# Loads and stores of the first tile spread over two DMA queues, and picks and gathers moved

## The chip, the cores and the metric

The kernel runs on one core of a Trainium2 chip. The metric is the device time of one execution in microseconds (us), lower is better. On the core TensorE (PE) multiplies matrices, VectorE (DVE) and GpSimd (POOL) do elementwise work, ScalarE (ACT) copies and applies functions, and SyncE (SP) only issues DMAs. ScalarE and GpSimd issue DMAs too. DMAs that SP issues appear in the profile as queue q1, those of ScalarE as q10, the gathers of GpSimd as q0.

## The reference

A recommendation tower: 32 embedding tables are looked up for 1024 rows, three layers of a compressed interaction network run over them, and a small dense network follows.

```python
e = stack([tbl_m[ids[:, m]] for m in range(32)], axis=1)       # B=1024, M=32, D=16
x0 = xk = e
for W in (W0, W1, W2):                                         # (32, 32 or 64, 64)
    xk = relu(einsum('bmd,bhd,mhk->bkd', x0, xk, W))           # (B, 64, D)
    outs.append(sum(xk, axis=2))
h = concatenate(outs + [dense_ctx], axis=1)                    # (B, 208)
h = relu(h @ W_top1 + b_top1); h = relu(h @ W_top2 + b_top2)
y = h @ W_top3
```

All arithmetic is in float32.

## The kernel before, in words

The batch is cut into eight tiles of 128 rows (i = 0 to 7), each tile into two sides (A and Bs) of 64 rows. A **phase** is one layer of one side of one tile, written (i, layer, side). The list PHASES (line 59) sets the order of all phases on all engines: (0,0,A), (0,1,A), (0,0,Bs), (0,2,A), (0,1,Bs), (1,0,A), (0,2,Bs), (1,0,Bs), (1,1,A), (1,1,Bs), (1,2,A), (2,0,A), (1,2,Bs), (2,0,Bs), (2,1,A) and so on.

A phase is a row of **steps**. In a step VectorE multiplies a 128 x 1024 tile: the previous layer's values, which ScalarE has laid into two pairs of PSUM banks (xk, one for each of two "turns"), by one **slot** of x0rep, which holds rows of x0 repeated over partitions (line 1119). TensorE then multiplies the product z by a piece of the layer's weights and adds it up in a PSUM bank acc (line 768). A phase of layer 0 has four steps, which use slots 0, 1, 2 and 1 again (in (0,0,A) in the order 0, 2, 1, 1); one of layer 1 or 2 has sixteen, which use the slots 0 to 7 twice. Of those sixteen, two to five products are made by GpSimd (line 569) into z_pool. VectorE's products go round a ring of six buffers (RING), GpSimd's round one of four: a product waits until TensorE is through with the step that had its buffer. When a phase is over, ScalarE takes acc as relu into xk_copy (line 870) and layer_out (line 876), VectorE sums layer_out over d (line 1092), and xk_copy feeds the next layer of the same side (lines 832, 851, 856). In layer 0 TensorE adds squares times w0d ahead of the last step (line 764); the squares are loaded as rows of x0 (load_rows, line 426) and squared by ScalarE (line 812).

**How x0 gets there.** The embeddings of a tile are gathered into emb[:, i % 2] (128 rows x 32 x 16). SP stores them to the DRAM buffer x0_rows, and loads from there the slots (load_x0, line 433, 512 KB each), the layouts lay (load_lay, line 420, 512 KB each) and the rows (load_rows, 128 KB). For tile 0 this is done by halves, even and odd embeddings (save_first, line 461): a half is stored by two DMAs, of 16 and of 8 rows of emb, in pieces of 64 bytes, 3072 in all. Side A's slots 0, 2, 4 and 6 are loaded behind the even half, slots 1, 3, 5 and 7 behind the odd one. For tile 0, side A, the layouts aren't loaded; TensorE turns and selects the rows (turn_rows, select_rows), with a copy by ScalarE between them (copy_rows, line 791, one for each half). Later tiles: save_x0 (line 412), then load_side (line 440) for A and Bs. x0rep has three groups of eight slots, used in turn by the sides.

**Gathers.** Most embeddings come by indirect DMAs that GpSimd issues (line 518). Those of tiles 0 and 1 stand at the start; those of tiles 2 to 7 stand between its products, so many a phase as later_gathers (line 141) says: 6 or 10 a phase, and by the table IN_PHASE (line 137) for tile 2: 4 in (0,1,A), 6 in each of (0,2,A), (0,1,Bs) and (0,2,Bs), 5 in each of (1,1,A) and (1,1,Bs). Of tiles 0 and 1 some embeddings from small tables are **picked** instead: the tables are loaded whole, TensorE multiplies them by one-hot matrices, and VectorE masks and sums (pick_rows, line 1056). There are ten picks, 0 to 9, six of them for tile 0. Picks 0 to 6 stand ahead of the phases on VectorE; the table `between` (line 1088) puts number 7 ahead of step 1 of phase (0,0,A), number 8 ahead of its step 2 and number 9 ahead of phase (0,1,A).

**Weights.** w0 is loaded in 16 small DMAs. w1 and w2 are loaded by ScalarE's queue (load_w, line 777) in eight straight DMAs (STRAIGHT: four pieces of two; 64 KB or 32 KB each) and in four of 32 KB (WRAPPED) from a DRAM copy with wrapped rows, w1_wrap or w2_wrap. The copies are made from DRAM to DRAM by two DMAs of 128 KB each (make_wrap, line 382). TensorE starts phase (0,1,A) when all twelve w1 loads have landed, and (0,2,A) when all of w2 have. The w2 loads stand in ScalarE's program behind the second fill of phase (0,1,A) and wait there for slot 7 and for w2_wrap.

**ScalarE's order in the opening:** table loads; w0 loads; copy_rows(0); four w0 loads; straight w1 pieces 0 and 1; copy_rows(1); pieces 2 and 3; square(0, A); the w1_wrap loads; then the phases. **SP's order:** save_first(0); two w0 loads; slots 0, 2, 4, 6; two w0 loads; save_first(1); wait for it; slot 1; rows; slots 3, 5, 7; make_wrap for w2; load_side(0, Bs), which is rows, a layout, slots 0 and 1, a layout, slots 2 to 7; the dense network's weights (about 0.9 MB); then tile 1.

Each engine works through its own program in order, so a DMA issue that waits holds everything behind it on that engine.

Of the kernel before, what the change touches and what calls it, by code (L numbers as in the profile page):

```python
# [17 lines left out]
P = 128  # L18
# [118 lines left out]
IN_PHASE = {(0, 1, A): 4, (0, 2, A): 6, (0, 1, Bs): 6, (0, 2, Bs): 6, (1, 1, A): 5, (1, 1, Bs): 5}  # L137
# [63 lines left out]
FIRST_SAVES = 4  # L201
# [10 lines left out]
def build(nc, ids, ctx_t, tables, sel, ident, w0a, w0b, w0d, w1, w2, wt1, bt1, wt2, bt2, wt3, out):  # L212
    with ExitStack() as stack:
# [89 lines left out]
        saved_first = sem("saved_first")  # L303
# [83 lines left out]

        def load_lines(queue, by_act, g):

            for m in of_group(g)[0]:  # L390
                if (m in LOADED_BY_ACT) == by_act:
                    queue.dma_start(lines[:, ALL_PICKED.index(m), 0:per_line(m) * D],
                                    tables[m].rearrange("(p j) d -> p (j d)", p=LINES)).then_inc(lines_in[g], 16)

        @block.sync
        def _(sp):
# [20 lines left out]
            def columns(i, side):  # L417
                return (i * SIDES + side) * WIDE

# [12 lines left out]

            def load_x0(i, side, slot):

                g = (i * SIDES + side) % X0_GROUPS
                src = bass.AP(x0_rows, slot * PITCH + columns(i, side),
                              [[2 * PITCH, GROUPS], [0, PER_GROUP], [1, WIDE]])
                sp.dma_start(x0rep[:, g, slot, :], src).then_inc(x0_in[g][slot], 16)

            def load_side(i, side):  # L440
# [8 lines left out]
                for slot in range(SLOTS):  # L449

                    bi, bs = divmod(i * SIDES + side - X0_GROUPS, SIDES)
                    if bi >= 0:
                        sp.wait_ge(z_ready, slot_users(bi, bs, slot, "dve", DVE_COUNT))
                        used = slot_users(bi, bs, slot, "pool", POOL_COUNT)
                        if used:
                            sp.wait_ge(z_pool_ready, used)
                    load_x0(i, side, slot)
                    if slot == 1 and i == 0:
                        load_lay(i, side, 1)

            def save_first(odd):

                sp.wait_ge(gathered_first[odd], 16 * len(FIRST_GATHERS[odd]))
                sp.wait_ge(picked_out, PICKED_EVEN if odd == 0 else len(PICKED))
                for lo, hi, row in ((0, M, odd), (0, X_ROWS - M, M + odd)):
                    dst = bass.AP(x0_rows, row * PITCH, [[D, P], [2 * PITCH, (hi - lo) // 2], [1, D]])
                    sp.dma_start(dst, emb[:, 0, lo + odd:hi:2, :]).then_inc(saved_first, 16)

            save_first(0)
            sp.wait_ge(w0_twice_in, 32)  # L470
            load_w0(sp, W0_LOADS, W0_LOADS + 2)
            sp.wait_ge(saved_first, 32)
            for slot in range(0, SLOTS, 2):
                load_x0(0, A, slot)
            load_w0(sp, W0_LOADS + 2, TILES0 * P // M)
            save_first(1)
            sp.wait_ge(saved_first, 64)
            for slot in range(1, SLOTS, 2):
                load_x0(0, A, slot)
                if slot == 1:  # L480
                    load_rows(0, A)
            make_wrap(sp, w2_wrap, w2, w2_wrap_in)
# [33 lines left out]
        def _(pool):  # L516
# [23 lines left out]
            def gather_later(j, m):  # L540

                if m == 0:

                    if j == 2:
                        pool.wait_ge(idx_in, 16)
                        pool.wait_ge(saved_first, 16 * FIRST_SAVES)
# [229 lines left out]
        def _(act):  # L776
# [27 lines left out]
            load_w(w1_sb, w1.tensor, TILES, w1_in, STRAIGHT[:2])  # L804
            copy_rows(1)
            load_w(w1_sb, w1.tensor, TILES, w1_in, STRAIGHT[2:])
# [9 lines left out]
            load_w(w1_sb, w1_wrap, WRAP, w1_in, WRAPPED)  # L816

# [162 lines left out]
        def _(dve):  # L980
# [104 lines left out]
            between = {1: 7, 2: 8, 4: 9}  # L1085
# [10 lines left out]
            for n, (i, layer, side) in enumerate(PHASES):  # L1096
                g = i * SIDES + side
                filled = [False, False]
                if n == 1:
                    pick_rows(between[len(STEPS[0])])  # L1100
# [6 lines left out]
                for c, (k, (_, _, bank, other)) in enumerate(mine):  # L1107
                    count = DVE_COUNT[n, k]
                    if n == 0 and k in between:
                        pick_rows(between[k])  # L1110
# [81 lines left out]
```

## Time and profile before

| | us |
|---|---|
| median of 3 runs (lowest, highest) | 632.28 (631.21, 635.13) |
| the profiled execution | 633.34 |
| its span | 631.5 |
| VectorE busy in the span | 577.9 (92%) |
| TensorE busy in the span | 586.0 (93%) |
| GpSimd busy in the span | 497.1 (79%) |
| ScalarE busy in the span | 349.7 (55%) |
| mean DMA rate over the span | 151 GB/s |
| granted TensorE clock, mean | 0.97 |

All rows come from the one profiled execution, and times in them count from its span's start. Matmul ends are modelled, so a busy TensorE is not TensorE at its peak. A row of a timeline is: start us, duration us, engine, line, operation, out <- in, shapes, count, and in brackets the idle time ahead of it with what ended it. Rows that follow one another on an engine are merged, so the start of a merged row is that of its first instruction. "SPq" and "ACTq" rows are DMA issues: their duration is the engine's time for issuing, not the transfer. A wait put down to a DMA may have had several semaphores; the one that came last is named.

### The profile page before, as it was taken

Reading aid. Unit: us, or ns where it says so; the run is one execution under the profiler, and the core shown is the slowest. Engines: PE = TensorE matmul, PEld = TensorE weight load, DVE = VectorE, ACT = ScalarE, POOL = GpSimd, SP = SyncE. Lnnn points to the kernel's source line nnn. Section 1 sums busy time; section 2 is a strip of 40 time slices with the busy share of each in tenths; the row PEclk is TensorE's granted clock in tenths of the full one; section 3 lists DMA queues with packets and bytes.
Section 4 is the critical chain, followed back from the end, with each engine's and each line's share of the span. In section 5 each row is a group of like instructions: output and inputs, shape, how many; then the busy total and the mean of one; then the engine's idle time right before and its main releaser. Section 6 shows DMA issues by size and latency. Waiting matters only on the chain.

```text
span 631.5 us, 8730 instructions
## 1 busy us (share of the span) xinstructions
PE 586.0 (93%) x3126; PEld 215.7 (34%) x3126; DVE 577.9 (92%) x582; ACT 349.7 (55%) x535; POOL 497.1 (79%) x349
## 2 busy tenths in 40 slices
PE   3852789999999999999999999999999999999998
PEld 3730222222343224323343224322343224333444
DVE  6746669899999999999999999999999999999993
ACT  0105165455766657535766657536756666756741
POOL 6753549899988998899888988898888896568770
PEclk8796699999999999999999999999999999999999
DMA  4789979990399918995499927992599838950000
GB/s 107 139 162 234 225 126 226 237 229 3 34 237 246 209 5 158 235 233 97 53 237 230 207 17 174 254 247 38 93 234 235 164 27 224 294 167 1 1 2 2
DMA packets 89342, 95.36 MB, mean 151 GB/s; under 512 B 59613, under 2 KB 68354, under 8 KB 89298
## 3 DMA queue, kind: packets, MB, share of 16 engines
q1 hardware_dynamic: 79086, 91.06, 63.9%
q0 software_dynamic: 7104, 1.83, 4.3%
q10 hardware_dynamic: 3108, 1.90, 1.2%
q8 instruction: 25, 0.41, 0.3%
q14 instruction: 19, 0.16, 0.1%
HBM read 91.35 MB, written 3.94 MB: 151 GB/s over the span
## 4 chain that ended last, share of the span: by engine, by line
PE 25%; DVE 23%; issue 5%; ACT 1%; DVEq 0%
PE acc L768 22%; DVE z L1119 22%; DVE row_sums L1092 1%; PE top L605 1%; ACT xk L832 0%; ACT xk L851 0%; PE top L596 0%; PE top L593 0%; PE acc L764 0%; ACT xk L856 0%; PE acc L645 0%; PE xk L633 0%; PE xk L625 0%; PE top L580 0%; DVEq L1117 0%
## 5 line engine op out<-in xcount | busy, mean ns | idle before, releaser
L1119 DVE TENSOR_TENSOR z<-xk,x0rep 128x1024 f32<-128x1024 f32 x457 | 523.7, 1236 | 30.3 <-DMA x0rep<-x_rows 9.5
L768 PE MATMUL acc<-z,w_sb 128*64 128x512 f32 x1828 | 434.5, 601 | 31.0 <-DMA w_sb<-w_wrap 15.0
L569 POOL TENSOR_TENSOR z_pool<-x0rep,xk_copy 128x1024 f32<-128x1024 f32 x119 | 283.3, 2381 | 59.4 <-PE acc L768 41.1
L518 POOL DMA_INDIRECT emb<-tbl,idx x222 | 212.9, 959 | 58.7 <-issue 48.5
L768 PEld LDWEIGHTS acc<-z,w_sb 128*64 128x64 f32 x1828 | 124.6, 137 | 306.0 <-issue 165.3
L856 ACT ACTIVATE xk<-xk_copy 32x1024 f32<-32x1024 f32 x128 | 130.5, 1019 | 92.9 <-DVE z L1119 88.4
L768 PE MATMUL acc<-z_pool,w_sb 128*64 128x512 f32 x476 | 122.6, 593 | 0.4 <-POOL z_pool L569 0.4
L870 ACT ACTIVATE xk_copy<-acc 64x512 f32<-64x512 f32 x128 | 75.2, 588 | 8.2 <-PE acc L768 6.7
L851 ACT ACTIVATE xk<-lay 128x1024 f32<-128x1024 f32 x15 | 15.4, 1028 | 75.3 <-DVE z L1119 75.3
L768 PEld LDWEIGHTS acc<-z_pool,w_sb 128*64 128x64 f32 x476 | 33.8, 137 | 65.7 <-issue 62.1
L832 ACT ACTIVATE xk<-xk_copy 128x1024 f32<-128x1024 f32 x31 | 31.9, 1028 | 14.1 <-DVE z L1119 13.7
L1092 DVE TENSOR_REDUCE row_sums<-layer_out 128x32 f32<-128x512 f32 x47 | 32.8, 697 | 0.0
L812 ACT ACTIVATE squares<-squares 32x1024 f32<-32x1024 f32 x16 | 16.8, 1050 | 28.7 <-DMA squares<-x_rows 16.0
L876 ACT ACTIVATE layer_out<-acc 128x512 f32<-128x512 f32 x47 | 27.8, 591 | 2.7 <-PE acc L768 1.9
L888 ACT ACTIVATE in<-row_sums 64x32 f32<-64x32 f32 x94 | 21.3, 227 | 4.1 <-DVE row_sums L1092 3.1
L677 PE MATMUL acc<-x0rep 125*128 125x160 f32 (+1 forms) x68 | 15.2, 394 | 6.3 <-DMA x0rep<-tbl 6.3
L832 ACT ACTIVATE xk<-lay 128x1024 f32<-128x1024 f32 x15 | 15.4, 1028 | 4.2 <-DMA lay<-x_rows 4.0
L764 PE MATMUL acc<-squares,w0d_sb 128*64 128x512 f32 x64 | 17.5, 625 | 0.3
L677 PEld LDWEIGHTS acc<-x0rep 125*128 125x128 f32 x68 | 13.3, 272 | 8.8 <-DMA x0rep<-tbl 6.8
L605 PEld LDWEIGHTS top<-h,wt_sb 128*64 128x64 f32 x224 | 12.7, 137 | 4.0 <-issue 4.0
L1039 DVE TENSOR_TENSOR x0rep<-acc,mask 128x480 f32<-128x480 f32 (+1 forms) x10 | 6.6, 665 | 7.7 <-PE acc L677 7.7
L605 PE MATMUL top<-h,wt_sb 128*64 128x128 f32 x224 | 13.4, 273 | 0.0
(67 smaller groups left out, 126.5 us busy)
## 6 DMA issues: line engine op xcount, KB each, us to landing
x0rep<-x_rows SPq DMA_DIRECT2D x128, 512.0 KB, 20.8
lay<-x_rows SPq DMA_DIRECT2D x30, 512.0 KB, 7.0
emb<-tbl,idx POOLq DMA_INDIRECT x222, 3.6
squares<-x_rows SPq DMA_DIRECT2D x16, 128.0 KB, 20.5
x_rows<-emb SPq DMA_DIRECT2D x7, 256.0 KB, 4.6
x_rows<-emb SPq DMA_DIRECT2D x9, 128.0 KB, 6.3
w_wrap<-w SPq DMA_DIRECT2D x4, 128.0 KB, 9.7
w_sb<-w ACTq DMA_DIRECT2D x8, 64.0 KB
```

The costliest lines, as they stand in the source:

```text
L518: pool.indirect_dma_start(out=emb[:, i % 2, m, :], out_offset=None, in_=tables[m], in_offset=bass.IndirectOffsetOnAxis(ap=idx[:, i, m:m + ...
L569: pool.tensor_mul(z_pool[:, (count - 1) % POOL_RING, :], x0rep[:, g % X0_GROUPS, slot, :], xk_copy[:, side, :]).then_inc(z_pool_ready, 1)
L605: last = pe.matmul(top[halves[half], m * P:(m + 1) * P], wt2_sb[:, k, columns_of(m, half)], h1[:, k, :], start=(k == 0), stop=(k == F1 // ...
L677: op = pe.matmul(acc[:, ACC_AT[q], t * n * D:(t + 1) * n * D], hots[:, q % HOTS, t * P:(t + 1) * P], lines[:, ALL_PICKED.index(m), 0:n * D ...
L768: mm = pe.matmul(bank[c * H:(c + 1) * H, :], w[:, tile, :], src[:, c * COLS:(c + 1) * COLS], start=(k == 0), stop=last)
L832: act.activation(xk[:, 0, :], src, ACT.Copy).then_inc(xk_ready[0], 1)
L856: op = act.activation(xk[q * Q:(q + 1) * Q, 1, :], xk_copy[other * Q:(other + 1) * Q, side, :], ACT.Copy)
L870: op = act.activation(xk_copy[half * H:(half + 1) * H, side, c * COLS:(c + 1) * COLS], bank[c * H:(c + 1) * H, :], ACT.Relu)
L876: act.activation(layer_out[:, n % OUTS, :], bank, ACT.Relu).then_inc(acc_taken, 1)
L888: op = act.activation(dst[:, at:at + ROWS], row_sums[c * H:(c + 1) * H, i % 2, row, :], ACT.Copy)
L1092: dve.tensor_reduce(row_sums[:, i % 2, SUM_ROWS.index((layer, side)), :], layer_out[:, n % OUTS, :].rearrange("p (b d) -> p b d", d=D), AX ...
L1119: dve.tensor_mul(z[:, (count - 1) % RING, :], xk[:, bank, :], src).then_inc(z_ready, 1)
```

## The change

It has five parts.

1. save_first takes the queue as an argument, and the semaphore saved_first becomes one for each half. The odd half is stored from ScalarE's queue, behind straight w1 pieces 0 and 1 and ahead of copy_rows(1).
2. Slots 1 and 3 of side A are loaded from ScalarE's queue, behind copy_rows(1) and a wait for the odd store, ahead of straight w1 pieces 2 and 3. SP loads slots 0, 2, 4 behind the even store; then, behind the odd store, the rows and slots 5, 6, 7.
3. make_wrap for w2 moves from SP (behind slot 7) to ScalarE, behind the w1_wrap loads, which follow square(0, A).
4. Pick 8 goes ahead of phase (0,1,A), pick 9 ahead of its step 4.
5. The gathers of tile 2: none in (0,1,A), 7 instead of 5 in each of (1,1,A) and (1,1,Bs).

```diff
-IN_PHASE = {(0, 1, A): 4, (0, 2, A): 6, (0, 1, Bs): 6, (0, 2, Bs): 6, (1, 1, A): 5, (1, 1, Bs): 5}
+IN_PHASE = {(0, 1, A): 0, (0, 2, A): 6, (0, 1, Bs): 6, (0, 2, Bs): 6, (1, 1, A): 7, (1, 1, Bs): 7}
...
-        saved_first = sem("saved_first")
+        saved_first = [sem(f"saved_first{odd}") for odd in range(2)]
...
+        def save_first(queue, odd):
+
+            queue.wait_ge(gathered_first[odd], 16 * len(FIRST_GATHERS[odd]))
+            queue.wait_ge(picked_out, PICKED_EVEN if odd == 0 else len(PICKED))
+            for lo, hi, row in ((0, M, odd), (0, X_ROWS - M, M + odd)):
+                dst = bass.AP(x0_rows, row * PITCH, [[D, P], [2 * PITCH, (hi - lo) // 2], [1, D]])
+                queue.dma_start(dst, emb[:, 0, lo + odd:hi:2, :]).then_inc(saved_first[odd], 16)
...
-            save_first(0)
+            save_first(sp, 0)
             sp.wait_ge(w0_twice_in, 32)
             load_w0(sp, W0_LOADS, W0_LOADS + 2)
-            sp.wait_ge(saved_first, 32)
-            for slot in range(0, SLOTS, 2):
-                load_x0(0, A, slot)
+            sp.wait_ge(saved_first[0], 32)
+            for slot in (0, 2, 4):
+                load_x0(sp, 0, A, slot)
             load_w0(sp, W0_LOADS + 2, TILES0 * P // M)
-            save_first(1)
-            sp.wait_ge(saved_first, 64)
-            for slot in range(1, SLOTS, 2):
-                load_x0(0, A, slot)
-                if slot == 1:
-                    load_rows(0, A)
-            make_wrap(sp, w2_wrap, w2, w2_wrap_in)
+
+            sp.wait_ge(saved_first[1], 32)
+            load_rows(0, A)
+            for slot in (5, 6, 7):
+                load_x0(sp, 0, A, slot)
             load_side(0, Bs)
...
             load_w(w1_sb, w1.tensor, TILES, w1_in, STRAIGHT[:2])
+            save_first(act, 1)
             copy_rows(1)
+            act.wait_ge(saved_first[1], 32)
+            for slot in (1, 3):
+                load_x0(act, 0, A, slot)
             load_w(w1_sb, w1.tensor, TILES, w1_in, STRAIGHT[2:])
...
             square(0, A)
             act.wait_ge(w1_wrap_in, 32)
             load_w(w1_sb, w1_wrap, WRAP, w1_in, WRAPPED)
+            make_wrap(act, w2_wrap, w2, w2_wrap_in)
...
-            between = {1: 7, 2: 8, 4: 9}
+            between = {(0, 1): 7, (1, 0): 8, (1, 4): 9}
...
                 if n == 1:
-                    pick_rows(between[len(STEPS[0])])
+                    pick_rows(between[1, 0])
...
-                    if n == 0 and k in between:
-                        pick_rows(between[k])
+                    if (n, k) in between and (n, k) != (1, 0):
+                        pick_rows(between[n, k])
```

## Rows read from the trace of the kernel before

**Rows 1.** The page: busy time of each engine, share and instructions.
```profile
PE 586.0 (93%) x3126; PEld 215.7 (34%) x3126; DVE 577.9 (92%) x582; ACT 349.7 (55%) x535; POOL 497.1 (79%) x349
```

**Rows 2.** Windows: length, busy of PE, PEld, DVE, ACT, POOL, clock, DMA, GB/s.
```profile
67.00:73.00 6.00, 5.96 (x16) 1.93 (x18) 2.99 (x3) 0.00 (x0) 5.36 (x5) 0.51 1.06 231
73.00:84.00 11.00, 11.00 (x54) 3.97 (x52) 9.35 (x9) 3.19 (x4) 0.02 (x1) 1.00 1.07 219
...
124.00:160.00 36.00, 34.44 (x154) 10.15 (x156) 36.00 (x35) 21.30 (x27) 33.35 (x22) 1.00 0.52 118
```

**Rows 3.** Timeline of VectorE, the opening and around 190 us.
```profile
48.01 2.35 DVE L1119 TENSOR_TENSOR z<-xk,x0rep 128x1024 f32<-128x1024 f32 x2 [8.56 <-DMA x0rep<-x_rows]
50.29 0.65 DVE L1039 TENSOR_TENSOR x0rep<-acc,mask 128x480 f32<-128x480 f32 x1
50.97 0.95 DVE L1052 TENSOR_REDUCE emb<-x0rep 128x48 f32<-128x480 f32 x1
53.67 1.42 DVE L1103 TENSOR_SCALAR xk<-acc 64x512 f32<-64x512 f32 x2 [1.75 <-PE acc L768]
55.13 4.62 DVE L1119 TENSOR_TENSOR z<-xk,x0rep 128x1024 f32<-128x1024 f32 x4
62.44 2.35 DVE L1119 TENSOR_TENSOR z<-xk,x0rep 128x1024 f32<-128x1024 f32 x2 [2.69 <-issue]
...
87.96 2.36 DVE L1119 TENSOR_TENSOR z<-xk,x0rep 128x1024 f32<-128x1024 f32 x2 [5.39 <-ACT xk L832]
...
182.38 18.21 DVE L1119 TENSOR_TENSOR z<-xk,x0rep 128x1024 f32<-128x1024 f32 x16
```

**Rows 4.** Timeline of SP's DMA issues, 25 to 43 us.
```profile
29.85 9.07 SPq L467 DMA_DIRECT2D x_rows<-emb  x2
42.66 0.55 SPq L438 DMA_DIRECT2D x0rep<-x_rows  x1
```

**Rows 5.** DMA issues, us to landing: windows 21:24, 32:34 and 42:43.2.
```profile
x_rows<-emb SPq DMA_DIRECT2D x1, 64.0 KB, 3.8
...
x_rows<-emb SPq DMA_DIRECT2D x1, 64.0 KB, 12.2
...
x0rep<-x_rows SPq DMA_DIRECT2D x1, 512.0 KB, 5.3
```

**Rows 6.** Timeline of TensorE, start of phase (0,1,A).
```profile
67.03 7.41 PE L768 MATMUL acc<-z,w_sb 128*64 128x512 f32 x20 [13.41 <-DMA w_sb<-w_wrap]
```

**Rows 7.** Timeline of ScalarE and its DMA issues.
```profile
27.23 2.75 ACTq L785 DMA_DIRECT2D w_sb<-w  x4
...
48.70 2.68 ACTq L785 DMA_DIRECT2D w_sb<-w_wrap  x4
...
63.29 8.95 ACTq L785 DMA_DIRECT2D w_sb<-w_wrap  x4
...
83.92 2.40 ACT L870 ACTIVATE xk_copy<-acc 64x512 f32<-64x512 f32 x4 [5.19 <-PE acc L768]
...
187.05 1.03 ACT L851 ACTIVATE xk<-lay 128x1024 f32<-128x1024 f32 x1 [4.48 <-DVE z L1119]
```

**Rows 8.** DMA queues (packets, MB, engine share): windows 38:42, 54:65, 65:85.
```profile
q10 hardware_dynamic: 258, 0.23, 19.1%
...
q1 hardware_dynamic: 915, 2.52, 99.8%
q10 hardware_dynamic: 147, 0.14, 5.8%
...
q10 hardware_dynamic: 411, 0.36, 8.5%
```

**Rows 9.** Timeline of GpSimd.
```profile
86.45 2.37 POOL L569 TENSOR_TENSOR z_pool<-x0rep,xk_copy 128x1024 f32<-128x1024 f32 x1 [13.43 <-PE acc L768]
...
163.56 0.98 POOL L518 DMA_INDIRECT emb<-tbl,idx  x1 [0.16 <-issue]
168.38 0.94 POOL L518 DMA_INDIRECT emb<-tbl,idx  x1 [0.30 <-issue]
```

**Rows 10.** SP's slot loads for tile 2, and the first one's landing (window 174:174.5).
```profile
174.02 5.41 SPq L438 DMA_DIRECT2D x0rep<-x_rows  x8
...
x0rep<-x_rows SPq DMA_DIRECT2D x1, 512.0 KB, 8.7
```

More of the change, by code:

```diff
@@ L200 @@
 FIRST_GATHERS = [[m for m in GATHERED[0] if m % 2 == odd] for odd in range(2)]
-FIRST_SAVES = 4
 W0_LOADS = 12
@@ L386, in make_wrap, with columns, load_x0 @@
                                 src[:, t:t + WRAP // 2, :].rearrange("p t k -> p (t k)")).then_inc(done, 16)
+        def columns(i, side):
+            return (i * SIDES + side) * WIDE
+        def load_x0(queue, i, side, slot):
+            g = (i * SIDES + side) % X0_GROUPS
+            src = bass.AP(x0_rows, slot * PITCH + columns(i, side),
+                          [[2 * PITCH, GROUPS], [0, PER_GROUP], [1, WIDE]])
+            queue.dma_start(x0rep[:, g, slot, :], src).then_inc(x0_in[g][slot], 16)
+        def save_first(queue, odd):
[4 more added lines that the diff above has]
+                queue.dma_start(dst, emb[:, 0, lo + odd:hi:2, :]).then_inc(saved_first[odd], 16)
         def load_lines(queue, by_act, g):
@@ L415, in save_x0 @@
                 sp.dma_start(dst, emb[:, i % 2, lo:hi, :]).then_inc(done, 16)
-            def columns(i, side):
-                return (i * SIDES + side) * WIDE
             def load_lay(i, side, n):
@@ L431, in load_rows @@
                              bass.AP(x0_rows, columns(i, side), [[PITCH, M], [1, WIDE]])).then_inc(rows_in[side], 16)
[L433 to L438, printed above, removed]
             def load_side(i, side):
@@ L456, in load_side @@
                             sp.wait_ge(z_pool_ready, used)
-                    load_x0(i, side, slot)
+                    load_x0(sp, i, side, slot)
                     if slot == 1 and i == 0:
                         load_lay(i, side, 1)
[L461 to L467, printed above, removed]
-            save_first(0)
+            save_first(sp, 0)
             sp.wait_ge(w0_twice_in, 32)
             load_w0(sp, W0_LOADS, W0_LOADS + 2)
-            sp.wait_ge(saved_first, 32)
-            for slot in range(0, SLOTS, 2):
-                load_x0(0, A, slot)
+            sp.wait_ge(saved_first[0], 32)
+            for slot in (0, 2, 4):
+                load_x0(sp, 0, A, slot)
             load_w0(sp, W0_LOADS + 2, TILES0 * P // M)
-            save_first(1)
-            sp.wait_ge(saved_first, 64)
-            for slot in range(1, SLOTS, 2):
-                load_x0(0, A, slot)
-                if slot == 1:
-                    load_rows(0, A)
-            make_wrap(sp, w2_wrap, w2, w2_wrap_in)
+            sp.wait_ge(saved_first[1], 32)
+            load_rows(0, A)
+            for slot in (5, 6, 7):
+                load_x0(sp, 0, A, slot)
             load_side(0, Bs)
@@ L545, in gather_later @@
                         pool.wait_ge(idx_in, 16)
-                        pool.wait_ge(saved_first, 16 * FIRST_SAVES)
+                        for odd in range(2):
+                            pool.wait_ge(saved_first[odd], 32)
                     else:
```

## The prediction

> **What bounds the kernel now.** I read the page first, then the windows, then each engine's timeline of the opening, then the DMA queues of short windows.
>
> From about 124 us on VectorE is the limit: between 124 and 160 us it is busy for all 36.00 us, and over the whole span for 577.9 us of 631.5 although the opening leaves it idle [rows 1, 2]. So a change in the opening shifts everything behind it one for one. The chain of waits doesn't reach back into the opening, so that is read from the engines' rows.
>
> In the opening VectorE has two products of the first phase (layer 0, side A) done, waits 8.56 us for slot 1 of x0 and goes on at 48.01 [rows 3]. That slot was issued by SP at 42.66, when the odd rows' store had landed. The store was issued at 29.85 behind four x0 loads in SP's queue; SP stood in its two issues for 9.07 us [rows 4], and the second half needed 12.2 us to land where that of the even rows had needed 3.8 [rows 5].
>
> The second wait is the larger one. VectorE starts layer 1's first phase at 55.13 [rows 3], but TensorE starts it at 67.03, after 13.41 us of idling that a load from w1_wrap ended [rows 6]. From there on TensorE is the limit: its clock is granted at 0.51 from 67 to 73 us (the 1.2 GHz level, after the idle stretch), at 1.00 behind it [rows 2]; VectorE stands between single products and waits for it, and its next run of products starts only at 87.96 [rows 3], after ScalarE has taken that phase's sums from 83.92 on [rows 7]. So **when w1 is complete sets the start of everything: 87.96 is 67.03 plus 20.93**.
>
> Why is it complete so late? The four w1_wrap loads of 32 KB each were issued at 48.70 [rows 7]. ScalarE's queue q10 moved 0.14 MB from 54 to 65 us, which is these four, while SP's queue moved 2.52 MB; then 0.36 MB in 20 us, which is most of the eight w2 loads behind them (384 KB) [rows 8]. So beside a full SP queue **a load on ScalarE's queue costs 11/4 = 2.7 us, whether it has 32 or 64 KB**: about the 2.3 us that one 0.52 MB slot of SP's takes at 229 GB/s, plus itself. The two queues take turns. The four w1 loads before them (the third and fourth pieces of the straight part, issued behind copy_rows(1)) had it better: SP's large loads were through, and q10 moved 0.23 MB in the 4 us from 38 to 42 [rows 8].
>
> **The change part by part.**
>
> (a) The odd rows' store moves to ScalarE's queue, ahead of copy_rows(1). ScalarE is free at 29.98 (27.23 + 2.75) [rows 7]. Alone it would land 3.8 us later, at 33.8; beside SP's slots it waits behind four w1 loads and the even slots' turns. With slot 6 taken out of the even group SP's large loads end one slot, 2.3 us, earlier. Best bound 33.8, worst 42.7 (as now). I take 40.4 = 42.7 - 2.3, because 3072 rows of 64 bytes still have to follow the w1 loads in their own queue once SP's slots are through. A stall in issuing the second half, as on SP, would end by then; it would hold copy_rows(1), which is not needed before slot 1.
>
> (b) Slots 1 and 3 go on ScalarE's queue, beside SP's rows and slots 5, 6, 7. Slot 1 alone took 5.3 us from issue to landing [rows 5], so 3.0 us beside its own 2.3. Taking turns it costs 4.6, so it lands at 40.4 + 3.0 + 4.6 = 48.0. VectorE's 48.01 doesn't move, nor do the end of the first phase and 55.13. Bounds: 2.3 us less if ScalarE's queue is served first, 2.3 more if it is served last.
>
> (c) On that queue slots 1 and 3 now stand before four straight w1 loads, and these before the four w1_wrap loads. All eight run beside a full SP queue: it has rows, three slots, side Bs's ten large loads and the top weights, at 229 GB/s over 30 us from about 41. Sum: 40.4 + 3.0 + 2 x 4.6 + 8 x 2.65 = **73.8 us for the last w1 load, against 67.03: 6.8 us later**. Bounds: if ScalarE's queue were served first, the ten loads would move in 7 us and TensorE would start as soon as VectorE lets it; with 2.9 us a load and the store at 42.7 it is 78. I stay near 2.7 because two long stretches show it.
>
> Behind it nothing changes in the chain: TensorE is cold after its idling as now, the six products of VectorE's ring wait as now, 20.93 us follow.
>
> (d) make_wrap for w2 moves from SP past the squares to ScalarE's queue: two DRAM to DRAM copies, behind all of (c). Two turns, 5.4 us: w2_wrap is ready at about 79. ScalarE waits for it in order ahead of square(0, Bs) and the fills of phase (0, 0, Bs). Now four issues that can't be placed hold it for 8.95 us from 63.29 on [rows 7]; then it is free at about 84, five us behind w2_wrap. VectorE, at most its ring of six ahead of TensorE, is through with phase 1 six products (6.8 us) before ScalarE takes the sums, so at 77.1 now and 83.9 then. Fills that come a few tenths late are covered by TensorE, which has phase 1 to finish until 90.7. So I price this at nothing; without that cover it is a rival.
>
> (e) Picks: number 8 takes the place of number 9 ahead of layer 1's first phase, in the wait before 53.67. Number 9 (0.65 + 0.95 us) goes behind four products, where VectorE stands still for 2.69 us until 62.44 (ScalarE's second fill), and later waits for TensorE [rows 3]: nothing. Worst case 1.6 us.
>
> (f) Gathers: four leave phase (0, 1, A), two each go to (1, 1, A) and (1, 1, Bs). What they leave is no gain: POOL then waits 13.43 us for the sums anyway [rows 9]. What they join is full: of 124 to 160 us POOL is busy for 33.35 [rows 2], and the rest are the gaps around gathers. A gather behind another costs 0.94 us and a gap of 0.30, 1.25 in all [rows 9], so tile 2's last one, now at 163.56, goes 5.0 us later against VectorE. SP's store, its row load and its slots (from 174.02) follow it [rows 9, 10]. Slot 0 landed at 174.0 + 8.7 = 182.7 [rows 10], slots 1 and 2 at 2.2 us each behind, so 187.1 for slot 2. The products that need slots 0, 1 and 2 start at about 187.1, 188.2 and 189.3: the second bank's fill at 187.05 [rows 7] is released by the last product of the phase before, and a product takes 18.21/16 = 1.14 [rows 3]. So slot 2 has 2.2 us of room, and 5.0 later it costs **2.8 us**. The POOL products of (1, 2, A) come late for TensorE in the same place, by at most the 5.0; VectorE's ring of six products, 6.8 us, holds that. Bounds: 0 and 5.0. In the later tiles the gather plan is as now and VectorE is 2.8 later, so it isn't paid twice.
>
> Sum: 6.8 + 2.8 = 9.6. The profiled execution took 633.34 (its span 631.5), 1.06 over the median 632.28. So 633.34 + 9.6 = 642.9 by its clock, 641.9 by the median. I take 641.5.
>
> The Trainium skill (DMA: Bandwidth & Descriptors, "Issuing engines are not separate DMA queues") says that DMAs of different engines run on the same 16 and interleave, and that a second issuer only saves issue time. By that rule moving loads changes little: w1 would be complete at 67 again and only (f) would be left, some 635. It speaks against a gain, and [rows 8] agree as to the taking of turns; the same page ("Why a DMA increments its semaphore by 16 and not by 1") gives a load of few rows to few of the engines, which fits that 32 KB cost as much as 64.
>
> **Rivals.**
>
> 1. **The share is better than I price it**: ScalarE's loads get more than a turn for a turn, or the store lands at 36 to 38, and w1 is complete between 64 and 70. Then (c) is -3 to +3, (f) stays: 632 to 638, middle 635. For it: 4 KB pieces on q10 are shown by no row. Against: eleven and twenty microseconds at one rate. Chance 0.25.
>
> 2. **Faster**: w1 complete by 57. Then VectorE sets phase 1: its eight products from 62.44 end at 71.6, TensorE's end at 73.4 against 83.9. That is -10.5 + 2.8 = -7.7: 624.6. It is decided by whether ten loads land within 17 us of the store; by [rows 8] they need 33. Chance 0.08.
>
> 3. **ScalarE held by w2_wrap**: the copy comes last in its queue, behind SP's large loads, the w2 loads can't be placed, and the fills for (0, 0, Bs) come at 90 or later. Then the sums of phase 1 are taken late too: 4 us more, 646. For it: the 8.95 us of issue now. Chance 0.17.
>
> My forecast holds 0.50.
>
> **Numbers.** Within 1%, what a measurement of this kernel can tell from no change, is 626 to 638.6. Faster by more 0.09 (rival 2 and a little), within 0.26 (rival 1), slower 0.65. The forecast's own range is 637 to 646. With rivals 1 and 3 the range is 632 to 649.
>
> **What would show it.** The issue of save_first on ScalarE at about 30 and its landing near 40.4; slot 1's product near 48; TensorE's first product of layer 1 near 74 behind a w1_wrap load, VectorE's next long run near 94.8; w2_wrap landing near 79 and ScalarE's square near 84; at (2, 0, A), some 10 us later than now, VectorE waiting about 3 us for x0. The prediction is wrong if w1 is complete before 67, or if the w1_wrap loads take less than 2 us each beside SP's.

## The result, and the profile after

| | before | after |
|---|---|---|
| median, us (lowest, highest) | 633.17 (631.21, 635.13) | 643.42 (640.11, 645.15) |
| ratio, 95% interval | | 1.0156 (1.0132, 1.0181) |
| the profiled execution | 633.34 | 645.15 |
| its span | 631.5 | 643.3 |

The change costs 10 us. The prediction was 641.5 us, and it gave a slowdown of more than 1% a chance of 0.65. (The kernel before has one run more here than in the table of the first part, hence 633.17 and not 632.28.) Line numbers have moved: products L1119 to L1122, multiplications L768 to L766, w loads L785 to L783, slot loads L438 to L395, the store L467 to L403, gathers L518 to L515, ScalarE's take of acc L870 to L873.

The page after: VectorE, the limit over most of the span, is busy for 578.1 us against 577.9 in [rows 1], so the 11.8 us by which the span has grown are waiting.

```profile
PE 589.7 (92%) x3126; PEld 217.0 (34%) x3126; DVE 578.1 (90%) x582; ACT 349.7 (54%) x535; POOL 496.7 (77%) x349
```

The windows that answer to [rows 2] (length, busy of PE, PEld, DVE, ACT, POOL, clock, DMA, GB/s):

```profile
67.00:72.50 5.50, 0.00 (x0) 0.00 (x0) 0.00 (x0) 0.00 (x0) 0.00 (x0) 0.50 1.05 232
72.80:79.00 6.20, 6.20 (x18) 2.08 (x20) 3.31 (x3) 0.00 (x0) 0.00 (x0) 0.59 1.09 254
```

From 67.0 to 72.5 us nothing computes while the DMA engines move 232 GB/s. The granted clock is 0.50 there (the 1.2 GHz level; TensorE has been idle since 50.5) and 0.59 on the mean of the 6.2 us behind it, where [rows 2] have 0.51.

ScalarE with its DMA issues, to be read against [rows 7]:

```profile
30.45 6.26 ACTq L403 DMA_DIRECT2D x_rows<-emb  x2
36.75 1.01 ACT L791 ACTIVATE lay<-xk 16x1024 f32<-16x1024 f32 x1 [10.66 <-issue]
39.24 1.25 ACTq L395 DMA_DIRECT2D x0rep<-x_rows  x2
40.52 2.84 ACTq L783 DMA_DIRECT2D w_sb<-w  x4
43.43 2.60 ACTq L783 DMA_DIRECT2D w_sb<-w_wrap  x4
46.05 2.11 ACTq L384 DMA_DIRECT2D w_wrap<-w  x2
...
76.92 2.60 ACTq L783 DMA_DIRECT2D w_sb<-w_wrap  x4
...
80.06 1.06 ACT L814 ACTIVATE squares<-squares 32x1024 f32<-32x1024 f32 x1 [20.80 <-issue]
...
89.30 2.40 ACT L873 ACTIVATE xk_copy<-acc 64x512 f32<-64x512 f32 x4 [4.88 <-PE acc L766]
```

The odd store is issued at 30.45 and has landed at 39.24, when the slots behind its wait go out: 3.4 us before the 42.66 of [rows 4]. The w1_wrap loads are issued at 43.43, 5.3 us before the 48.70 of [rows 7]. Yet TensorE's first product of layer 1 is later than in [rows 6], behind one of them:

```profile
72.79 7.03 PE L766 MATMUL acc<-z,w_sb 128*64 128x512 f32 x20 [22.26 <-DMA w_sb<-w_wrap]
```

VectorE, against [rows 3]:

```profile
44.76 2.36 DVE L1122 TENSOR_TENSOR z<-xk,x0rep 128x1024 f32<-128x1024 f32 x2 [1.99 <-DMA x0rep<-x_rows]
...
52.05 4.62 DVE L1122 TENSOR_TENSOR z<-xk,x0rep 128x1024 f32<-128x1024 f32 x4
...
59.35 2.35 DVE L1122 TENSOR_TENSOR z<-xk,x0rep 128x1024 f32<-128x1024 f32 x2 [1.11 <-ACT xk L859]
74.81 1.23 DVE L1122 TENSOR_TENSOR z<-xk,x0rep 128x1024 f32<-128x1024 f32 x1 [13.10 <-PE acc L766]
...
93.34 9.14 DVE L1122 TENSOR_TENSOR z<-xk,x0rep 128x1024 f32<-128x1024 f32 x8 [5.39 <-ACT xk L835]
```

What the change aims at it does: slot 1's product starts 3.25 us sooner and layer 1's first four products 3.1 sooner. All of it, and 5.4 us more, is lost in front of TensorE; 93.34 stands against 87.96.

The second loss is around 190 us. The rows are GpSimd's last gather for tile 2, SP's slots (as in [rows 9, 10]), the landing of the first slot (window 184 to 184.8), and VectorE:

```profile
173.97 0.98 POOL L515 DMA_INDIRECT emb<-tbl,idx  x1 [0.16 <-issue]
```

```profile
184.25 5.25 SPq L395 DMA_DIRECT2D x0rep<-x_rows  x8
```

```profile
x0rep<-x_rows SPq DMA_DIRECT2D x1, 512.0 KB, 9.5
```

```profile
193.92 1.23 DVE L1122 TENSOR_TENSOR z<-xk,x0rep 128x1024 f32<-128x1024 f32 x1 [1.52 <-DMA x0rep<-x_rows]
196.05 1.23 DVE L1122 TENSOR_TENSOR z<-xk,x0rep 128x1024 f32<-128x1024 f32 x1 [0.91 <-DMA x0rep<-x_rows]
198.20 11.40 DVE L1122 TENSOR_TENSOR z<-xk,x0rep 128x1024 f32<-128x1024 f32 x10 [0.92 <-PE acc L766]
```

The third of these waits is put down to TensorE, which itself stood still for 2.17 us, until 196.74, for GpSimd's last product of (1,2,A). By the trace's completion events slot 2 landed at 198.08, 0.1 us before VectorE went on, so the slot and TensorE ended that wait together.

The same instruction in two kernels shows how the distance grows. VectorE's row sums, first before, then after:

```profile
181.79 0.70 DVE L1092 TENSOR_REDUCE row_sums<-layer_out 128x32 f32<-128x512 f32 x1
200.48 0.70 DVE L1092 TENSOR_REDUCE row_sums<-layer_out 128x32 f32<-128x512 f32 x1
222.01 0.72 DVE L1092 TENSOR_REDUCE row_sums<-layer_out 128x32 f32<-128x512 f32 x1
293.40 0.68 DVE L1092 TENSOR_REDUCE row_sums<-layer_out 128x32 f32<-128x512 f32 x1
552.85 0.68 DVE L1092 TENSOR_REDUCE row_sums<-layer_out 128x32 f32<-128x512 f32 x1
```

```profile
187.20 0.68 DVE L1095 TENSOR_REDUCE row_sums<-layer_out 128x32 f32<-128x512 f32 x1
209.53 0.68 DVE L1095 TENSOR_REDUCE row_sums<-layer_out 128x32 f32<-128x512 f32 x1
232.04 0.68 DVE L1095 TENSOR_REDUCE row_sums<-layer_out 128x32 f32<-128x512 f32 x1
303.97 0.68 DVE L1095 TENSOR_REDUCE row_sums<-layer_out 128x32 f32<-128x512 f32 x1
563.37 0.68 DVE L1095 TENSOR_REDUCE row_sums<-layer_out 128x32 f32<-128x512 f32 x1
```

The differences are 5.4, 9.05, 10.0, 10.6 and 10.5 us. The spans differ by 11.8: in this execution 1.9 us more come at tile 7, where a slot lands late for VectorE, and 0.6 go in its last wait.

### The profile page after: what moved, and what is told of

It is laid out like the page before. It is cut to its first block and busy times, and to the rows that moved or that the text cites. A ratio compares the mean times of both kernels' runs of the same rounds, so it can differ in the third digit from the quotient of the medians.

```text
span 643.3 us, 8731 instructions
## 1 busy us (share of the span) xinstructions
PE 589.7 (92%) x3126; PEld 217.0 (34%) x3126; DVE 578.1 (90%) x582; ACT 349.7 (54%) x535; POOL 496.7 (77%) x349
## 5 line engine op out<-in xcount | busy, mean ns | idle before, releaser
L1122 DVE TENSOR_TENSOR z<-xk,x0rep 128x1024 f32<-128x1024 f32 x457 | 523.3, 1216 | 43.2 <-PE acc L766 18.5
L766 PE MATMUL acc<-z,w_sb 128*64 128x512 f32 x1828 | 435.5, 602 | 31.9 <-DMA w_sb<-w_wrap 22.3
L515 POOL DMA_INDIRECT emb<-tbl,idx x222 | 212.8, 959 | 56.7 <-issue 50.1
L766 PEld LDWEIGHTS acc<-z,w_sb 128*64 128x64 f32 x1828 | 125.1, 138 | 307.9 <-issue 176.8
L766 PE MATMUL acc<-z_pool,w_sb 128*64 128x512 f32 x476 | 123.0, 595 | 3.5 <-POOL z_pool L567 3.5
L873 ACT ACTIVATE xk_copy<-acc 64x512 f32<-64x512 f32 x128 | 75.3, 588 | 8.2 <-PE acc L766 6.7
L766 PEld LDWEIGHTS acc<-z_pool,w_sb 128*64 128x64 f32 x476 | 33.6, 137 | 69.2 <-issue 59.7
L879 ACT ACTIVATE layer_out<-acc 128x512 f32<-128x512 f32 x47 | 27.8, 591 | 2.1 <-PE acc L766 1.4
```

The costliest lines, as they stand in the source:

```text
L515: pool.indirect_dma_start(out=emb[:, i % 2, m, :], out_offset=None, in_=tables[m], in_offset=bass.IndirectOffsetOnAxis(ap=idx[:, i, m:m + ...
L766: mm = pe.matmul(bank[c * H:(c + 1) * H, :], w[:, tile, :], src[:, c * COLS:(c + 1) * COLS], start=(k == 0), stop=last)
L873: op = act.activation(xk_copy[half * H:(half + 1) * H, side, c * COLS:(c + 1) * COLS], bank[c * H:(c + 1) * H, :], ACT.Relu)
L879: act.activation(layer_out[:, n % OUTS, :], bank, ACT.Relu).then_inc(acc_taken, 1)
L1122: dve.tensor_mul(z[:, (count - 1) % RING, :], xk[:, bank, :], src).then_inc(z_ready, 1)
```

## The experiments

Theory A is the prediction's: w1 is late because its loads take turns with SP's large ones, so what stands ahead of them in ScalarE's queue sets the start of layer 1; the gathers are a loss of their own at (2,0,A). The runs were made on several chips. On two of them the kernel before takes 651 to 653 us, not 632; so each is compared with the kernel before on its own chip, and its trace with a trace of the same kind of chip.

**The gathers alone.**

```diff
-IN_PHASE = {(0, 1, A): 4, (0, 2, A): 6, (0, 1, Bs): 6, (0, 2, Bs): 6, (1, 1, A): 5, (1, 1, Bs): 5}
+IN_PHASE = {(0, 1, A): 0, (0, 2, A): 6, (0, 1, Bs): 6, (0, 2, Bs): 6, (1, 1, A): 7, (1, 1, Bs): 7}
```

> The kernel before with the new gather plan alone: none in (0,1,A), 7 each in (1,1,A) and (1,1,Bs). Theory A (the prediction's part f, resized by the trace after the change, where VectorE's sums fall back by 3.65 us at tile 2's side A, 0.98 at its side Bs and 0.5 in tile 3): 3 to 5.5 us slower than before, all of it behind 180 us, with VectorE waiting for slots of x0 at (2,0,A). Rival B (what is lost behind 180 us comes from the loads moved to the other queue): no change, within 1 us.

Measured: ratio 1.0075 (1.0042, 1.0109), +4.9 us. Its VectorE at (2,0,A):

```profile
205.16 1.22 DVE L1119 TENSOR_TENSOR z<-xk,x0rep 128x1024 f32<-128x1024 f32 x1 [0.91 <-issue]
207.28 1.23 DVE L1119 TENSOR_TENSOR z<-xk,x0rep 128x1024 f32<-128x1024 f32 x1 [0.89 <-DMA x0rep<-x_rows]
209.17 2.35 DVE L1119 TENSOR_TENSOR z<-xk,x0rep 128x1024 f32<-128x1024 f32 x2 [0.67 <-DMA x0rep<-x_rows]
```

VectorE waits in the same place as after the whole change and for as long in all: 3.2 us with the 0.75 for TensorE that follow, 3.35 there. The front is as before. The gathers' loss stands by itself.

**The change with the gathers of before** (the same line the other way round).

> The changed kernel with the gather plan of before. Theory A: only the late w1 is left, 5.4 us over the kernel before (about 638.5), TensorE starting layer 1 near 72.8 us, no shift behind 180 us. Rival B: it stays at the changed kernel's 643.

Measured: 1.0152 (1.0101, 1.0203), 9.9 us on a chip with the longer opening. VectorE goes through (2,0,A) with one wait of 0.35 (the kernel before has 0.46 there on such a chip). In its opening the straight w1 pieces and all behind them go out at 60.8, as the odd store has landed at 59:

```profile
93.55 7.43 PE L766 MATMUL acc<-z,w_sb 128*64 128x512 f32 x20 [20.77 <-DMA w_sb<-w_wrap]
```

That is 34.7 us behind the store's landing; the kernel with the gathers alone has 24.3 (60.96 to 85.23). The direction is A's, the size above the 5.4 expected. The whole change was never run on a chip with the longer opening, so how its 10 us divide into front and gathers is read from its own rows, and this run shows only that the front loses without the new gathers.

**Straight w1 pieces ahead of slots 1 and 3**, rest as in the last one.

```diff
             copy_rows(1)
+            load_w(w1_sb, w1.tensor, TILES, w1_in, STRAIGHT[2:])
             act.wait_ge(saved_first[1], 32)
             for slot in (1, 3):
                 load_x0(act, 0, A, slot)
-            load_w(w1_sb, w1.tensor, TILES, w1_in, STRAIGHT[2:])
```

> The changed kernel with the gather plan of before, and the third and fourth straight pieces of w1 issued ahead of the wait for the odd store and of slots 1 and 3. Theory A (a load on ScalarE's queue costs a turn of 2.65 us beside a full SP queue): two slots and four w1_wrap loads are left behind the store, 39.2 + 3.0 + 9.2 + 4 x 2.65 = 62.0 for the first TensorE product of layer 1 instead of 72.8; w2 is then the next to be late (layer 2's first product not before 85), so 2 to 5 us faster than the kernel before's 633, about 8 under the changed kernel with old gathers. Rival C (the turns don't matter; what is late is ScalarE itself, held by its store and waits): TensorE's start stays near 72 and the time near 638.

Measured: 1.0165 (1.0119, 1.0211), no gain. ScalarE's issue of the four straight loads, and VectorE:

```profile
58.25 2.78 ACTq L783 DMA_DIRECT2D w_sb<-w  x4
...
78.44 2.35 DVE L1122 TENSOR_TENSOR z<-xk,x0rep 128x1024 f32<-128x1024 f32 x2 [15.68 <-DMA x0rep<-x_rows]
```

Now slot 1, issued at 61.07 behind four small loads, lands 17 us later, and TensorE starts layer 1 at 92.88 all the same, 35.4 us behind the store's landing at 57.5. The edit did not do what the expectation counted on: copy_rows(1) held the four straight loads until 58.25, 0.7 us behind that landing, so all ten loads ran beside SP's large ones again, only in another order. Whatever is last in ScalarE's queue is late.

**Slots 1 and 3 back on SP's queue**, the store still on ScalarE's, gathers as before.

```diff
-            act.wait_ge(saved_first[1], 32)
-            for slot in (1, 3):
-                load_x0(act, 0, A, slot)
...
+            load_x0(sp, 0, A, 1)
             load_rows(0, A)
-            for slot in (5, 6, 7):
+            for slot in (3, 5, 6, 7):
```

> The changed kernel with the gathers of before and with slots 1 and 3 back on SP's queue (slot 1 right behind the odd store); the odd rows' store stays on ScalarE's queue, the straight w1 pieces 2 and 3 follow copy_rows(1) at once. Theory A (place in ScalarE's queue: each load that stands ahead of the w1_wrap loads beside a full SP queue costs a turn of 2.7 us, a slot 4.6): two slots fewer stand ahead of w1, so TensorE starts layer 1 within 2 us of the kernel before, and the time is 649 to 654 where before has 651.4 and the version with slots 1 and 3 on ScalarE's queue 662. Theory B (the store's 3072 rows of 64 bytes on ScalarE's queue are the loss): the loss stays, 659 to 663.

Measured: 1.0017 (0.998, 1.0054), 655.3 us; the kernel before 652.8. Theory B is out: the store by itself is not the loss, and with the two slots gone from ScalarE's queue the time is back (1.0152 with them). But the mechanism is not as clean as the time:

```profile
89.70 6.59 PE L767 MATMUL acc<-z,w_sb 128*64 128x512 f32 x20 [19.85 <-DMA w_sb<-w_wrap]
```

TensorE's start is 31.2 us behind the store's landing (58.49), where the gathers alone have 24.3: two slots fewer gave 3.5 us of the 9.2 that they were priced at. By the trace's completion events the first of the eight small loads, issued at 60.51, landed only at 69.4; from there to the last it took 2.9 us a load. What held the first one is open. The store itself landed earlier than in any trace that has it in SP's queue on such chips (58.49 against 60.96 to 68.80), which fits a time no worse than before, but the openings differ too much between executions to put a price on it.

**w1_wrap loads ahead of the square** in the kernel before.

```diff
-            square(0, A)
             act.wait_ge(w1_wrap_in, 32)
             load_w(w1_sb, w1_wrap, WRAP, w1_in, WRAPPED)
+            square(0, A)
```

> The kernel before with one edit: the w1_wrap loads stand ahead of square(0, A), so that they are issued near 36 us, when SP's large loads are through, and not at 48.7. Theory A: w1 is complete by 44 us, TensorE goes into layer 1 at about 56 without idling, its clock stays at full; w2 is then what is late, complete near 86; 6 to 9 us faster than before, about 625. Rival C: TensorE's idling moves on to another wait of the same length (w2, or the fills) and the time stays within 2 us of before.

Measured: 0.9977 (0.995, 1.0004), some 1.5 us: this is rival C's figure, and A's 6 to 9 us are not there. The w1 wait is gone and another stands behind it:

```profile
82.74 5.35 PE L768 MATMUL acc<-z,w_sb 128*64 128x512 f32 x16 [2.88 <-DVE z L1119]
...
113.57 4.49 PE L768 MATMUL acc<-z,w_sb 128*64 128x512 f32 x12 [4.81 <-DMA w_sb<-w_wrap]
```

The second row is (0,2,A): w2, whose loads go out only behind phase (0,1,A)'s second fill, is the next to be late. The same point in the first trace of the kernel before:

```profile
89.79 2.80 PE L768 MATMUL acc<-z,w_sb 128*64 128x512 f32 x12 [1.61 <-DMA w_sb<-w_wrap]
```

Counted from slot 1's issue (68.04 here, 42.66 before), TensorE starts layer 1 after 14.7 us and no longer after 24.4, but layer 2 after 45.5 for 47.1 (46.3 in the trace of the next run). So of 9.7 us gained for w1 at most 1.6 are left, about what the time shows.

**The kernel before once more**, on such a chip.

> The kernel before once more, for its rows on the chip on which the other experiments ran (median there 651.4 us against 632.3). Both theories expect the same: the second wait, TensorE idle for some 13 to 15 us ahead of layer 1's first phase with a w1_wrap load as its end, is there as on the first chip; the extra time is in the first 60 us, where VectorE and TensorE stand still and GpSimd's gathers go on.

Its 660.4 us are above the 652.8 median there. The w1 wait is 11.92 us at 92.42, a little below the 13 to 15 expected. The extra time is ahead of it, in front of table picks on VectorE:

```profile
31.54 0.69 DVE L1039 TENSOR_TENSOR x0rep<-acc,mask 128x512 f32<-128x512 f32 x1 [20.31 <-issue]
46.24 0.66 DVE L1039 TENSOR_TENSOR x0rep<-acc,mask 128x480 f32<-128x480 f32 x1 [12.41 <-remote]
```

**w1_wrap loads in SP's queue**, right behind slot 1, in the kernel before (load_w takes the queue as an argument).

```diff
                 if slot == 1:
+                    sp.wait_ge(w1_wrap_in, 32)
+                    load_w(sp, w1_sb, w1_wrap, WRAP, w1_in, WRAPPED)
                     load_rows(0, A)
...
-            act.wait_ge(w1_wrap_in, 32)
-            load_w(w1_sb, w1_wrap, WRAP, w1_in, WRAPPED)
```

> The kernel before with the four w1_wrap loads in SP's queue, right behind slot 1, instead of ScalarE's behind the square. Theory A (w1 is late because it takes turns with SP's large loads in another queue, not because of its bytes): in SP's own order the four loads of 32 KB cost SP under 3 us and w1 is complete before VectorE has its first product of layer 1, so TensorE's idle stretch ahead of layer 1 falls from about 14 us to under 5; the w2 loads on ScalarE's queue are the next to be late, at (0,2,A), and give a part of it back: 643 to 649 us against 651.4. Theory B (the rate of the DMA engines is the limit, whatever the queue): 650 to 653.

Measured: 0.9968 (0.9934, 1.0003), 650.0 us: between the two expectations, which as ratios to 651.4 are 0.987 to 0.996 and 0.998 to 1.002. So the time does not decide. The trace, of an execution of 659.2 us, tells more: TensorE's wait ahead of layer 1 is 2.87 us (for VectorE), and at (0,2,A) it waits for w2:

```profile
113.56 5.05 PE L784 MATMUL acc<-z,w_sb 128*64 128x512 f32 x12 [7.68 <-DMA w_sb<-w_wrap]
```

That is 45.7 us behind slot 1's issue at 67.81, again for 47.1 in the kernel before. The gain is there and w2 takes most of it back.

**w2's loads in SP's queue too.**

```diff
+                    make_wrap(sp, w2_wrap, w2, w2_wrap_in)
                     load_rows(0, A)
-            make_wrap(sp, w2_wrap, w2, w2_wrap_in)
+            load_w(sp, w2_sb, w2.tensor, TILES, w2_in, STRAIGHT)
...
+                    if slot == 3 and i == 0:
+                        sp.wait_ge(w2_wrap_in, 32)
+                        load_w(sp, w2_sb, w2_wrap, WRAP, w2_in, WRAPPED)
```

> The same with the w2 loads in SP's queue too: w2's wrapped copy made right behind the w1_wrap loads, the eight straight w2 loads behind slot 7, the four w2_wrap loads behind slot 3 of side Bs. Theory A: w2 is there before (0,2,A), ScalarE isn't held in its issues for 8.8 us, and nothing gives the gain back: 640 to 645 us against 651.4, and at least 2 us below the version with w1 alone. Theory B: no less than the version with w1 alone, 648 to 653, as side Bs's slots come later by what stands ahead of them.

Measured: 0.9878 (0.9824, 0.9933), 646.0 us, 4 below the version with w1 alone, as A has it (its 640 to 645 are 0.983 to 0.990 as ratios). Both waits are gone; TensorE's idle stretches over 1 us from layer 1 to 130 us are each ended by VectorE:

```profile
79.39 5.19 PE L788 MATMUL acc<-z,w_sb 128*64 128x512 f32 x16 [2.87 <-DVE z L1118]
86.61 1.08 PE L788 MATMUL acc<-z,w_sb 128*64 128x512 f32 x4 [2.03 <-DVE z L1118]
102.59 3.25 PE L788 MATMUL acc<-z,w_sb 128*64 128x512 f32 x12 [1.01 <-DVE z L1118]
```

The third row is (0,2,A), 37.9 us behind slot 1's issue at 64.67. The same bytes over the same engines: only the queue and the place in it differ. Which of the two it is these runs don't separate. w1's wait also went when its loads merely stood earlier in ScalarE's queue, and w2's loads were not tried early there.

**The change again, on another chip** (there the kernel before takes 632.5).

> The changed kernel itself, on the chip of the experiments, where the opening is some 19 us longer. If its two losses are independent, the front (1.0152 measured alone there, with the gathers of before) and the gathers (1.0075 alone) add up: a ratio of 1.022 to 1.024, 666 to 669 us where before has 652 to 653. If the later front gives the gathers room (VectorE late, so GpSimd has time), it stays at 1.015 to 1.018.

Measured: 1.0152 (1.0127, 1.0177), 641.8 us. It confirms the result, but the expectation was for a chip with the longer opening and is not tried by it. Row by row VectorE is 3.65 us behind at 97 to 182 us, 7.7 from 200 on: front 3.65, gathers 4.1 here.

**The odd store on ScalarE's queue and w1, w2 on SP's**: all that the change has in the first tile but slots 1 and 3 and the wrapped copy, with both groups of late loads on SP's queue (w2's twelve placed as in the version above; the excerpt leaves them out) and the old gathers.

```diff
             save_first(act, 1)
             copy_rows(1)
-            act.wait_ge(saved_first[1], 32)
-            for slot in (1, 3):
-                load_x0(act, 0, A, slot)
...
             sp.wait_ge(saved_first[1], 32)
+            load_x0(sp, 0, A, 1)
+            sp.wait_ge(w1_wrap_in, 32)
+            load_w(sp, w1_sb, w1_wrap, WRAP, w1_in, WRAPPED)
+            make_wrap(sp, w2_wrap, w2, w2_wrap_in)
             load_rows(0, A)
-            for slot in (5, 6, 7):
+            for slot in (3, 5, 6, 7):
```

> The version with w1's and w2's late loads in SP's queue, and beside it the odd rows' store on ScalarE's queue as in the change (slot 6 behind the odd store, slots 1 and 3 on SP's queue; picks as in the change, gathers as before). Theory A (the store alone is worth something: on the first chip it brought slot 1's product 3.25 us forward, and the loss came only from what stood in ScalarE's queue): 1 to 5 us below the version without it, a ratio to before of 0.980 to 0.987. Theory B (the store must wait behind four straight w1 loads and gains nothing where the gathers are the late part): 0.986 to 0.992, no difference.

Measured: **623.7 us, ratio 0.9868 (0.9845, 0.989)**, the fastest of all. The ratio lies in both expected ranges, and the version without the store was not run on this chip (0.9878 (0.9824, 0.9933) on another), so the time doesn't show that the store is worth anything beside the loads. VectorE:

```profile
45.08 2.36 DVE L1119 TENSOR_TENSOR z<-xk,x0rep 128x1024 f32<-128x1024 f32 x2 [1.93 <-DMA x0rep<-x_rows]
...
59.39 5.75 DVE L1119 TENSOR_TENSOR z<-xk,x0rep 128x1024 f32<-128x1024 f32 x5 [1.12 <-ACT xk L861]
...
73.45 2.36 DVE L1119 TENSOR_TENSOR z<-xk,x0rep 128x1024 f32<-128x1024 f32 x2 [2.06 <-DMA x0rep<-x_rows]
76.17 9.14 DVE L1119 TENSOR_TENSOR z<-xk,x0rep 128x1024 f32<-128x1024 f32 x8 [0.36 <-ACT xk L837]
```

76.17 stands against 87.96 before and 93.34 after. The order has a price too: at 73.45 VectorE waits 2.06 us for a slot of side Bs, which now stands behind the w1 and w2 loads in SP's queue. Between 126 and 131 us VectorE waits for slots again, 0.27, 1.02 and 0.62 us, and 9.6 of the 11.8 us are kept behind that (its row sum at 172.24 answers to 181.79).

**Three gathers moved the other way**, in the version with w1 and w2 on SP's queue.

```diff
-IN_PHASE = {(0, 1, A): 4, (0, 2, A): 6, (0, 1, Bs): 6, (0, 2, Bs): 6, (1, 1, A): 5, (1, 1, Bs): 5}
+IN_PHASE = {(0, 1, A): 4, (0, 2, A): 7, (0, 1, Bs): 7, (0, 2, Bs): 7, (1, 1, A): 4, (1, 1, Bs): 3}
```

> The version with w1's and w2's late loads in SP's queue, and beside it three of tile 2's gathers moved the other way: 7 instead of 6 in each of (0,2,A), (0,1,Bs) and (0,2,Bs), 4 and 3 instead of 5 and 5 in (1,1,A) and (1,1,Bs). Theory A (a gather in the full phases costs 1.25 us of the last gather's time against VectorE, and at (2,0,A) the kernel before waits for nothing, so only the losing side has a price): no gain, within 2 us of the version without it, ratio 0.984 to 0.991. Theory B (the loss is symmetric: fewer gathers late are worth as much as more cost): 3 us less, 0.979 to 0.984.

Measured: 0.9898 (0.9879, 0.9917), 626.1 us; no gain, as A has it, though the version without the moved gathers ran on another chip. It lost something in a new place:

```profile
118.15 9.14 DVE L1118 TENSOR_TENSOR z<-xk,x0rep 128x1024 f32<-128x1024 f32 x8 [4.39 <-ACT xk L836]
```

The version it is compared with waits 1.90 us there, and TensorE waits 1.12 us at 108.58 for a product of GpSimd's: the extra gathers hold these up, so there was no free room either. Ahead of the moved gathers, at its run in (0,2,A), VectorE is at 80.23 here and at 76.17 in the version with the store on ScalarE's queue, on the same chip: by these two traces the store and the picks of that version are worth 4.1 us there.

**The wrapped copy and the picks alone**, in the kernel before.

```diff
-            make_wrap(sp, w2_wrap, w2, w2_wrap_in)
...
             load_w(w1_sb, w1_wrap, WRAP, w1_in, WRAPPED)
+            make_wrap(act, w2_wrap, w2, w2_wrap_in)
...
-            between = {1: 7, 2: 8, 4: 9}
+            between = {(0, 1): 7, (1, 0): 8, (1, 4): 9}
```

> The kernel before with two parts of the change alone: w2's wrapped copy made from ScalarE's queue behind the w1_wrap loads, and pick 8 ahead of layer 1's first phase, pick 9 ahead of that phase's step 4. Theory A (both lie in time in which VectorE and ScalarE wait for w1 anyway): no change, a ratio of 0.997 to 1.003, VectorE's second long run of products as far behind TensorE's first product of layer 1 as before (20.9 us). Theory B (the copy comes last in ScalarE's queue, the w2 loads behind it hold ScalarE in its issues, and the fills of (0,0,Bs) come late): 3 to 5 us more, a ratio of 1.005 to 1.008, and a longer idle stretch of ScalarE ahead of the square.

Measured: 1.0023 (1.0003, 1.0043): 0.2 to 2.7 us more, within A's range. VectorE's run starts 21.0 us behind TensorE's start (90.09 and 69.07), as before's 20.9. Theory B is out.

## Why the prediction was right, point by point

(a) Odd store: 40.4 predicted, 39.24 measured. The issue stalled for 6.26 us and held copy_rows(1) until 36.75, as allowed for.

(b) Slot 1: predicted to land at 48.0, its product is at 44.76. It took 5.5 us from its issue, what it had taken alone on SP's queue [rows 5]; the turn I added (2.3) wasn't paid. The second slot and the eight loads beside a full SP queue do pay: from 44.76 to 72.79 they need 28.0 us, and 4.6 + 8 x 2.65 = 25.8 was the sum.

(c) w1: 73.8 predicted, 72.79 measured; +6.8 against +5.8. Two errors, slot 1 too dear and the rest too cheap, cancel in part; that is luck. The price of 2.7 us came from a wrong reading of [rows 8]: the 0.14 MB of 54 to 65 us are not just the four w1_wrap loads. By the trace's completion events these landed at 58.12, 60.90, 63.96 and 66.94, 2.94 us each, and the first began to move only at 54.79, 6.1 us behind its issue. After the change the eight loads landed between 52.76 and 72.70, 2.85 us apart, and 4.6 + 8 x 2.9 = 27.8 fits the 28.0. In the seven traces that have such loads beside a full SP queue the distance is 2.6 to 2.9 us.

The same events fit the equal price of 32 and 64 KB. Beside one that comes at its issue, a load of 32 KB has four completions at its end and one of 64 KB has eight, so if each stands for one DMA engine, an engine carries eight packets of 1 KB in either. Beside SP one such packet took 0.08 us and one of SP's, of 4 KB, 0.29 us, by the packets' own times in the trace of the kernel before. Taken in turns, packet by packet, that makes 8 x 0.37 = 3.0 us; this is an estimate, and the taking of turns by packets was not tried by a run.

Of the 5.8 us VectorE lost 5.4: TensorE's first 20 multiplications took 7.03 us for 7.41, at a granted clock of 0.59 for 0.51 on the mean.

(d), (e) Nothing was predicted, and 1.0023 (1.0003, 1.0043) was measured for both together, so little but perhaps not nothing. ScalarE was free at 80.06, four us sooner than I had worked out; rival 3 is out.

(f) Gathers: 5.0 us later against VectorE was exact: 173.97 - 163.56 = 10.4 = 5.4 + 5.0. The price was 2.8; it was 3.65 at (2,0,A), mostly because slot 0 took 9.5 us to land, not 8.7. That VectorE's ring holds GpSimd's late products was right only just: TensorE let VectorE go on no sooner than slot 2 did. Then +1.0 at side Bs and +0.5 at tile 3. "It isn't paid twice" was wrong: SP's queue keeps its lateness for another tile and a half. So **the mis-sized term is the gathers', 5.1 us for 2.8**; in the run by itself 4.9.

The sum: predicted 6.8 + 2.8 = 9.6, measured by rows 5.4 + 5.1 + 1.3 from tile 7 on = 11.8 in the profiled execution, 10.2 by the medians. One term came out too large and the other too small, so the time is nearer than its terms. In the other execution it is 3.65 + 4.1 + 0.2 = 8.0.

Rival 1 (w1 complete between 64 and 70) is out by the 72.79. Rival 2 failed in the change for the reason given. With w1 and w2 in SP's own order it comes true: a layer-1 start that VectorE sets was put at -10.5 us (without the gathers' 2.8), and 8.8 were measured with the store on ScalarE's queue as well. The Trainium skill (DMA: Bandwidth & Descriptors, "Issuing engines are not separate DMA queues") has the DMAs of two issuers run on the same engines and interleave, and a second issuer save only the time of issuing. The interleaving is what the rows show. What the prediction drew from it, that moving loads changes little, does not hold here: the place of small loads in the two queues was worth 5.8 us to lose and 8 (646.0 us at a ratio of 0.9878) to gain.

What stays open: why the first small load moves only some microseconds behind its issue (6.1 us in the kernel before), and why two of the chips need some 19 us more in the opening.

## What to carry to other kernels

A small load that something waits for did best in the queue of the large ones, ahead of those that can wait; behind them in time, in a second queue beside a full one, each took 2.6 to 2.9 us. Issuing it in the second queue before the large ones go out also took w1's wait away; for w2 that was not tried. Before a store or a slot is moved into a queue, list what stands behind it there and who waits for the last of it. And when a wait is taken away, look for the next one before counting the gain: here w2 stood behind w1 and took back most of it until both were moved.

## What had not been expected of the hardware

The same program takes 632 us on some chips and 651 to 653 on others, and the difference lies in the opening: in the slower trace slot 1 is issued at 68.80 for 42.66, which is 26.1 of the 27.1 us between the two spans (658.6 and 631.5; that execution is some 8 us above its chip's median). VectorE stands still for 20.31 and 12.41 us in the trace shown, where the first chip has no wait over 3.3 us up to 35 us, and TensorE for 14.24 and 12.67. The seven other traces from such chips each have one wait of 14 to 21 us there. Meanwhile the gathers' instructions keep their pace of 0.94 us and a gap of 0.30. SP's queue from 5 to 45 us (packets, MB, engine share), on the first chip and on the slower one:

```profile
q1 hardware_dynamic: 9729, 4.07, 50.1%
```

```profile
q1 hardware_dynamic: 2689, 1.39, 12.0%
```

No row names what the engines stood still for. From the second row sum to the tenth both traces need 84.77 us (97.02 to 181.79, and 121.84 to 206.61), so the ratios of the experiments there hold for the parts behind it, and less surely for the front.
